# Order of the first merges, loads and low parts in a conditioned-experts kernel on one core

## What is computed

```
hidden_i = x @ wi.T + 2 * (x @ common_wi_a.T) @ common_wi_b.T + 2 * (x @ A[e].T) @ B[e].T     # e: the batch's expert
hidden_i = relu(hidden_i)
hidden_o = hidden_i @ wo.T + 2 * (common, rank 16) + 2 * (expert e, rank 16)
x = x + mixture(hidden_o);  x = x + gated(project(x))
```

## Time and profile before

| | |
|---|---|
| median of 3 runs | 483.62 us (483.39 to 483.94) |
| the profiled execution | 483.61 us, its span 481.9 us |
| TensorE, ScalarE, VectorE, GpSimd busy | 99%, 82%, 80%, 24% |
| TensorE clock granted | full |

### The profile page before, as it was taken

The page is one execution under the profiler, slowest core; times in us unless marked ns, Lnnn a source line. Parts: engine busy times, 40 slices in busy tenths (PEclk is TensorE's granted clock), DMA queues, the critical chain, the costliest instruction groups (busy, mean ns, idle before and its releaser), DMA issues.

```text
span 481.9 us, 7478 instructions
## 1 busy us (share of the span) xinstructions
PE 476.3 (99%) x2270; PEld 396.2 (82%) x2270; DVE 387.9 (80%) x641; ACT 393.7 (82%) x542; POOL 117.2 (24%) x99
## 2 busy tenths in 40 slices
PE   8999999999999999999999999999999999999997
PEld 7998888888888888888888888888888888888885
DVE  4889899998889898988898898889897758554343
ACT  4889988888788898888888888888888888697743
POOL 3995212121212212121212121231313144400000
PEclk9999999999999999999999999999999999999999
DMA  7602702020210202020202012120202000000002
GB/s 214 211 6 90 284 1 89 0 90 8 82 52 35 88 0 88 0 88 0 88 1 87 32 56 84 48 89 0 88 2 88 2 0 0 1 0 1 0 23 69
DMA packets 7179, 26.31 MB, mean 55 GB/s; under 512 B 2226, under 2 KB 2610, under 8 KB 4978
## 3 DMA queue, kind: packets, MB, share of 16 engines
q1 hardware_dynamic: 5970, 21.73, 12.6%
q0 software_dynamic: 288, 2.88, 1.6%
q10 hardware_dynamic: 896, 1.38, 1.1%
HBM read 24.81 MB, written 1.18 MB: 54 GB/s over the span
## 4 chain that ended last, share of the span: by engine, by line
PE 97%; DMA 1%; SPq 1%; DVE 0%; issue 0%
PE bank L506 34%; PE bank L507 34%; PE bank L510 26%; PE bank L595 1%; PE bank L596 1%; DMA stage<-lora_all 1%; PE bank L528 1%; PE bank L525 0%; SPq L244 0%; PE bank L541 0%; SPq L257 0%; DVE act_out L1032 0%; DVE stage L1032 0%; DVE x L1283 0%; SPq L349 0%
## 5 line engine op out<-in xcount | busy, mean ns | idle before, releaser
L815 ACT ACTIVATE act_out<-bank,vec 128x512 f32<-128x512 f32 x256 | 165.5, 682 | 41.6 <-PE bank L510 31.7
L1122 DVE TENSOR_TENSOR hid_lo<-act_out,hid_hi 128x1024 fp32r<-128x1024 f32 x128 | 156.8, 1244 | 33.2 <-ACT hid_hi L820 33.1
L820 ACT ACTIVATE hid_hi<-act_out 128x1024 fp32r<-128x1024 f32 x128 | 136.0, 1062 | 8.0 <-PE bank L510 0.2
L469 POOL TENSOR_TENSOR cur<-cur,prod 128x512 f32<-128x512 f32 x48 | 65.1, 1356 | 237.3 <-DVE prod L1133 236.9
L506 PE MATMUL bank<-hid_hi,moe_hi 128*128 128x512 f32 x256 | 99.9, 390 | 0.0
L506 PE MATMUL bank<-xhi,moe_hi 128*128 128x512 f32 x256 | 99.7, 390 | 0.0
L510 PE MATMUL bank<-hid_hi,moe_lo 128*128 128x512 f32 x256 | 99.7, 390 | 0.0
L507 PE MATMUL bank<-hid_lo,moe_hi 128*128 128x512 f32 x256 | 99.7, 389 | 0.0
L507 PE MATMUL bank<-xlo,moe_hi 128*128 128x512 f32 x256 | 99.6, 389 | 0.0
L510 PE MATMUL bank<-xhi,moe_lo 128*128 128x512 f32 x256 | 99.6, 389 | 0.0
L506 PEld LDWEIGHTS bank<-hid_hi,moe_hi 128*128 128x128 f32 x256 | 48.1, 188 | 11.4 <-issue 0.2
(11 more groups left out here) (125 smaller groups left out, 566.3 us busy)
## 6 DMA issues: line engine op xcount, KB each, us to landing
cw_all<-cw_dram SPq DMA_DIRECT2D x16, 1024.0 KB, 4.6
stage<-ffn_w POOLq DMA_DIRECT2D x1, 2304.0 KB, 8.7
cw_all<-moe_w SPq DMA_DIRECT2D x4, 512.0 KB, 7.9
stage<-lora_all SPq DMA_DIRECT2D x5, 160.0 KB, 3.7
x<-x_t SPq DMA_DIRECT2D x3, 256.0 KB, 4.3
out_t<-x SPq DMA_DIRECT2D x3, 256.0 KB, 2.5
cur<-cond_base ACTq DMA_DIRECT2D x2, 256.0 KB, 3.3
stage<-ffn_w POOLq DMA_DIRECT2D x1, 512.0 KB, 3.8
```

The costliest lines, as they stand in the source:

```text
L469: pool.tensor_tensor(cur[:, c, :], cur[:, c, :], prod[:, s % 2, :], ALU.add).then_inc(add_done, 1)
L815: act.activation(act_out[:, f // 2, f % 2, :], bank[:, f, :], ACT.Gelu_apprx_tanh, bias=vec[:, V_B1 + e * FC + f:V_B1 + e * FC + f + 1]).t ...
L820: act.activation(hid_hi[:, s % 2, 2 * pr:2 * pr + 2, :], act_out[:, pr, :, :], ACT.Copy)\
L1122: dve.tensor_tensor(hid_lo[:, s % 2, 2 * pr:2 * pr + 2, :], act_out[:, pr, :, :], hid_hi[:, s % 2, 2 * pr:2 * pr + 2, :].bitcast(F32), ALU ...
```

## The change

- `MERGE_GROUPS` has (2,0),(3,0) second and (0,1),(1,1) third. By their places in the order, (2,0),(3,0) go to banks 4 and 5, and (0,1),(1,1) to 2 and 3.
- `first_load(queue, b)` issues batch `b`'s first half, then the whole of batch `b + 2`, then the second half. The separate loads of 2 and 3 go.
- The wait for the second halves moves to the third group. The two keep-warm products stand between groups 0 and 1. `WARM` is 12.
- The low part of (0,0) is GpSimd's first instead of VectorE's; its semaphore goes.
- `first_hidden` takes the place of `cond_hidden(0)`: the same twelve products, ordered by part (four hi·hi, four hi·lo, four lo·hi), with the wait for a part directly ahead of the products that need it.

```diff
 MERGE_GROUPS = (((0, 0), (1, 0)),
+                ((2, 0), (3, 0)),
                 ((0, 1), (1, 1)),
-                ((2, 0), (3, 0)),
                 ((2, 1), (3, 1)),
-LOWS = ((1, 0), (0, 1), (1, 1), (2, 0), ...
+LOWS = ((0, 0), (1, 0), (0, 1), (1, 1), (2, 0), ...
-WARM, KEEP_WARM = 13, 2
+WARM, KEEP_WARM = 12, 2
...
+        def half_load(queue, b, e, kind):
+            arrived = first_out_in[b] if kind else lora_in[b]
+            queue.dma_start(lora[lora_rows(b, kind), 0, :],
+                            lora_all[bass.ds(e, 1), 2 * RANK * kind:2 * RANK * (kind + 1), :]
+                            .rearrange("e r n -> (e r) n")).then_inc(arrived, 16)
+
         def first_load(queue, b):
             e = lora_expert(queue, b)
-            for kind, arrived in enumerate((lora_in[b], first_out_in[b])):
-                queue.dma_start(...).then_inc(arrived, 16)
+            half_load(queue, b, e, 0)
+            lora_load(queue, b + 2)
+            half_load(queue, b, e, 1)
...
             first_load(sp, 0)
-            lora_load(sp, 2)
             x_load(sp, 1)
...
+            merged_low(0, 0)
             merged_low(1, 0)
...
-                    pe.wait_ge(first_out_in[b] if j == 1 else lora_in[b], 16)
+                    pe.wait_ge(first_out_in[b] if j == 2 else lora_in[b], 16)
...
+            def first_hidden():
+                hi, lo, cols = mer_hi[:, 0, 0, :], mer_lo[:, 0, 0, :], batch_cols(0)
+                pe.wait_ge(mer_hi_done, HIGHS.index((0, 0)) + 1)
+                for weights, x in ((hi, xhi), (hi, xlo), (lo, xhi)):
+                    if x is xlo:
+                        pe.wait_ge(x0_split[0], 1)
+                    if weights is lo:
+                        pe.wait_ge(mer_lo_done, LOWS.index((0, 0)) + 1)
+                    for f in range(FC):
+                        mm = pe.matmul(bank[:, f // 2, (f % 2) * SEQ:(f % 2 + 1) * SEQ], weights[:, f * P:(f + 1) * P],
+                                       x[:, 0, cols], start=weights is hi and x is xhi and f % 2 == 0,
+                                       stop=weights is lo, skip_group_check=True)
+                mm.then_inc(cond_h_done, 1)
...
             merge_group(0)
+            warm(KEEP_WARM)
             merge_group(1)
-            warm(KEEP_WARM)
             merge_group(2)
             merge_group(3)
-            cond_hidden(0)
+            first_hidden()
             cond_hidden(1)
...
             act.wait_ge(ids_in, 16)
             first_load(act, 1)
-            lora_load(act, 3)
             base_load(act, 1)
...
             merged_sum(0, 0)
             merged_sum(1, 0)
-            first_low()
             merged_sum(0, 1)
```

More of the change, by code:

```diff
@@ L54 @@
          0), (5, 1), (6, 1), (7, 1))
-LOWS = ((1, 0), (0, 1), (1, 1), (2, 0), (3, 0), (2, 1), (4, 0), (4, 1), (3, 1), (5, 0), (6, 0), (7, 0), (5,
+LOWS = ((0, 0), (1, 0), (0, 1), (1, 1), (2, 0), (3, 0), (2, 1), (4, 0), (4, 1), (3, 1), (5, 0), (6, 0), (7, 0), (5,
         1), (6, 1), (7, 1))
@@ L193, in adaln_ffn @@
         merge_free = sem("merge_free")
-        mer_hi_done, mer_lo_done, first_lo_done = (sem(n) for n in ("mer_hi_done", "mer_lo_done", "first_lo_done"))
+        mer_hi_done, mer_lo_done = sem("mer_hi_done"), sem("mer_lo_done")
         moe_hi_done, moe_lo_done = sem("moe_hi_done"), sem("moe_lo_done")
@@ L251, in lora_load @@
             expert_load(queue, b, lora_expert(queue, b))
+        def half_load(queue, b, e, kind):
[3 more added lines that the diff above has]
+                            .rearrange("e r n -> (e r) n")).then_inc(arrived, 16)
         def first_load(queue, b):
             e = lora_expert(queue, b)
-            for kind, arrived in enumerate((lora_in[b], first_out_in[b])):
-                queue.dma_start(lora[lora_rows(b, kind), 0, :],
-                                lora_all[bass.ds(e, 1), 2 * RANK * kind:2 * RANK * (kind + 1), :]
-                                .rearrange("e r n -> (e r) n")).then_inc(arrived, 16)
+            half_load(queue, b, e, 0)
+            lora_load(queue, b + 2)
+            half_load(queue, b, e, 1)
         def x_load(queue, c):
@@ L475, in _ @@
             pool.wait_ge(mer_lo_done, len(LOWS))
-            pool.wait_ge(first_lo_done, 1)
             pool.wait_ge(cw_ready[0], 16)
@@ L551, in first_logits @@
                 logits(c, gate_bank(c))
+            def first_hidden():
[11 more added lines that the diff above has]
+                mm.then_inc(cond_h_done, 1)
             def cond_hidden(b):
[L554 to L557, removed]
+                pe.wait_ge(mer_lo_done, LOWS.index((b, 0)) + 1)
                 pe.wait_ge(x0_split[b // PER_CHUNK], 1)
@@ L1027, in merged_sum @@
                 if i >= SCRATCH:
[L1028 to L1031, removed]
+                    dve.wait_ge(mer_lo_done, LOWS.index(SUMS[i - SCRATCH]) + 1)
                 dve.scalar_tensor_tensor(merged(b, kind), bank[:, merge_bank(MERGED.index((b, kind))), :], COND_ALPHA,
                                          base[:, kind, :], ALU.mult, ALU.add).then_inc(merge_free, 1)
[L1035 to L1038, removed]
             def lang_lows(half):
```

## The result

The changed kernel takes 484.41 us (483.90 to 484.96, 11 runs), the one before 483.51 in the same sessions: a ratio of 1.0020, interval 1.0013 to 1.0028, 0.9 us slower. So the changed kernel is slower: the two medians give a loss of 0.4 and of 0.9 us, and the intervals together reach from nothing to 1.4 us. Single executions of both kernels spread over more than a microsecond. The profiled execution of the changed kernel took 484.08 us, one of its quicker ones.

A forecast was written before the change was run, and what follows sets the result against it. TensorE, busy 476.3 of 481.9 us, was taken as the bound, with gains only in its head. The 0.62 us won at batch 1 is given back at batch 2: 483.61 + 0.12 = 483.7, range 483.0 to 484.2.

The forecast's parts named there:

- What bounds the kernel, and where it decides: TensorE, 99% busy and gapless from 12.05 us; gains only ahead of that, decided by GpSimd's 0.38 us margin at batch 2.
- The filler, the first sums: Head: one filler less starts group 0 0.2 us earlier, at 5.98; GpSimd starts at 8.62.
- The loads: Input queues: output halves land between 7.6 and 8.8 us, taken as 8.0 because the same bytes had landed by 8.42.
- GpSimd's dense row: GpSimd from 8.62 us: operations every 1.25 us without gaps, (2,0) ending at 16.17 against 15.89, holding batch 2.
- rival 2: Output halves land late behind 160 KB: the bound from 8.75 us, over 0.97 us lost from 9.7 (484.6); chance 0.05.
- The price of the additional operation: GpSimd's row ahead of batch 2: the added low part of (0,0) costs 1.25 us there.
- VectorE's sums: VectorE in the head: sums every 0.60 us, off the path; (3,1) ends at about 12.7, group 4 wants it at 13.0.
- The restart: Batch 2's hidden half: first product 0.15 us after GpSimd's part ends, its successor another 0.07 us late.
- The range of the sum: Net effect at batch 2's start: +0.12 us, between −0.15 and +0.35.
- Rival 1: Gain stays: GpSimd's low part (2,0) is ready by 15.65, giving 483.0, 0.62 us faster; chance 0.09.
- The merges: TensorE ahead of batch 0: two output groups in a row take about 2.0 us, batch 0's hidden half at 10.0.
- Rival 3: VectorE slows GpSimd between 8.6 and 16.2 us, 0.44 us per meeting, two giving 484.6; chance 0.04.

The follow-up runs named there:

- the first kernel: The changed kernel with the old order of groups and the first low part on VectorE, new loads kept, against the kernel before: 486.18 us, ratio 1.0051.

## Why the prediction was wrong

I forecast 483.7, slower by 0.12 us, in a range to 484.2; it is 484.41. The sign was right, the size was not, and of the mechanism one half was: GpSimd's row does release batch 2, but what sets that row is the landing of the transfers and not the additional operation.

- *What bounds the kernel, and where it decides*: right. Behind batch 2's hidden half the work is the same and dense in both kernels. The stall of batch 1 went, but it came back ahead of batch 0 (0.81 us) and not as a wait of half a microsecond at batch 2. TensorE arrived there almost as late as GpSimd: the list of its waits has none on `ffn_lo`, and the first product came 0.22 us behind the one before it, where 0.12 is the pace without a wait.
- *The filler, the first sums*: a little better than costed. Group 0 started at 5.42 to 5.87, I had 5.98; GpSimd began at 8.43, I had 8.62.
- *The loads*, the step that failed: "All four transfers carry the same bytes that had landed by 4.72 + 3.7 = 8.42 before, which is why I take 8.0". The halves landed at 8.5 to 8.7. I had the upper end of that term at 8.8, took a value far from it, and never carried the upper end into the range: the sum let GpSimd's row hide a late landing. That an 80 KB half needed 3.5 to 3.7 us behind the 160 KB, against 2.6 in front of them, is what the equal bytes left out.
- *"The loads behind (chunk 1, the second base) keep their time"* is the same error: the second base landed at 9.2 to 10.5 instead of 8.9, and in two of four profiles it was the last thing that the sum of (0,1) waited for.
- *GpSimd's dense row* was therefore not dense. "The high parts that these need are ready by then" was wrong for (0,1) by 0.2 to 1.0 us. Where the base is in time, it is 2.6 to 2.7 us from group 2's start to GpSimd's start on (0,1). GpSimd ended (1,0) at about 10.95, so the row is tied to the landing from about 8.3 on, and not from 8.75 as rival 2 had it. By the constant distances in the table, what the landing loses from there the span loses too.
- *The price of the additional operation*: 1.25 us in GpSimd's row, right as a duration, nothing that the times resolve (1.0014 with it on VectorE). The gap ahead of (0,1) swallowed it. The Trainium skill's rule (GPSIMD Engine Reference, 4.1 Engine selection) of about twice the time fits the rows (1.29 against 0.69 us), and did not decide the case.
- *VectorE's sums* were said to be off the path, with (3,1) done at 12.7 for group 4 at 13.0. In the two profiles with the late base group 4 waited for (3,1), 0.2 and 0.6 us.
- *The restart*, 0.15 + 0.07 us: the first product came 0.05 or 0.06 us after GpSimd's part in all ten profiles in the table in which GpSimd released it, and the second about 0.1 us later than its pace (16.76 to 16.99 instead of 16.88). Together that is about 0.16 instead of 0.22, an error in the other direction.
- *The range of the sum* had its lower end wrong: with GpSimd done at 16.05, batch 2 proceeds as from 16.27, which is 0 and not −0.15. Rival 1's six operations would have to take 1.17 us each from 8.62 to 15.65, not 1.07. Neither changes the outcome.
- *The merges*, 2.0 us behind one another: right (8.69 to 10.67). That it cancels what the banks win was in the sum, but as part of a path that I held to be the shorter one.
- *Rival 1* (gain stays) fell. *Rival 3* (GpSimd slowed by VectorE) fell: its operations took 1.26 to 1.31 us up to 16.7. *Rival 2* comes nearest, with a smaller step than I gave it: it was priced to begin at 8.75, where no half landed, and to be worth a chance of 0.05. It had TensorE's own row alone, and neither the sum's wait for the base nor GpSimd's row behind it.

Not settled: why the second base lands 4.0 to 5.6 us after its issue with the new loads and 3.7 to 4.0 with the old ones (one old-load execution with late issues showed 5.4), though the same transfers stand ahead of it on both queues. How the loss divides is open too. An estimate from the table: batch 2 starts at 16.63 on average in the four profiles of the changed kernel and at 16.10 in the two before. The starts of group 2 and 7.79 us more would give 16.39, so about 0.3 us would be the halves with the longer row of merges, and about 0.2 the base. By the times, the run without the base's wait took back anything from none to half of the loss, and the order of the groups may cost something with the old loads as well.

## What to carry to other kernels

When a load is moved behind another, cost the whole chain from its landing at the late end of the range, and ask at which landing time the slack on every engine is used up. Here two rows, on TensorE and on GpSimd, were equally long from that moment on. Try the smallest edit that removes a stall first: here an exchange of banks with one low part moved (0.9989) was faster, while the same exchange inside five edits ended slower. And where single executions differ by more than the effect, read several: one profile of the changed kernel has a span of 482.0 us, against 481.9 in the first one of the kernel before.

## What the runs showed of the hardware

TensorE's clock fell in the head where the transfers made it wait. With the new loads and the old groups, TensorE stood for 1.16 us at 7.6 to 8.8, and then had half of its clock from about 10 to 13:

```profile
8.80 1.16 PE L532 MATMUL bank<-stage 32*128 32x128 f32 x16 [1.16 <-DMA stage<-lora_all]
9.89 1.14 PE L608 MATMUL bank<-blank 128*128 128x128 f32 x4
```

The columns of the windows are stretch, length, TensorE's busy time, its granted clock and the transfers' share and rate:

```profile
7.00:8.00 1.00, 0.64 (x4) 1.00 0.95 238
8.00:9.00 1.00, 0.20 (x2) 1.00 1.03 325
9.00:10.00 1.00, 1.00 (x17) 1.00 1.05 289
10.00:11.00 1.00, 1.00 (x8) 0.50 0.99 223
11.00:12.00 1.00, 1.00 (x15) 0.50 0.93 258
12.00:13.00 1.00, 1.00 (x15) 0.50 0.80 253
13.00:14.00 1.00, 1.00 (x11) 0.79 0.91 215
```

That is 1.2 GHz instead of 2.4. The profiles of the two kernels with the base ahead show the same, from between 11 and 12 us and from just before 10. By the mean clock of an execution (0.996 or less instead of 0.998 or more), it fell in all twelve executions of the first kernel, in seven of twelve with the base one place earlier, in four of six with the base first, in one of eleven of the new groups with old loads, in one of eleven of the changed kernel with (2,0) ahead (485.80 us), and in two of the 29 of the kernel before in one session (487.11 and 488.05 us). Against the median of the executions without a fall, for the first kernel that of the kernel before, it cost 1.2 to 4.5 us, more than anything that the change moves. The Trainium skill, page TensorE: Matmul & The Clock Gate, Part 1, describes these two levels and a fall after waits for transfers. The trace agrees, though the page's example has a longer wait in every round of a loop, and here one wait of 1.16 us stood ahead of the fall. None of the 22 timed executions of the changed kernel had it, so it is no part of the loss. The place of the keep-warm products between groups 0 and 1 may be what spared it; that wasn't tried by itself, and the kernels with the base ahead have them there too.

Single executions differ by their first transfers: with the new loads the second base took from 4.0 to 5.6 us at the same place of the program, group 0 started from 5.42 to 6.48, and the whole time spread by over a microsecond.
